# Moving GpSimd's C products, the step size's projection and the gate's Silu in a fused state-space layer

## The chip, the cores and the metric

The kernel runs on one core of a Trainium2 chip. It holds eight fused layers; the change is in the sixth part, a selective state space (Mamba-like). The metric is device time in microseconds for the whole kernel, lower is better, as the median of several runs. The core's engines are TensorE (PE; its weight loads are shown as PEld), VectorE (DVE), ScalarE (ACT), GpSimd (POOL) and SyncE (SP), which here only issues DMAs. Each engine works through its own program in order; they meet at semaphores.

## The reference, cut to what matters

The layer takes x (32 sequences of 256 positions, 128 features), normalizes it and does this:

```python
xz = xn @ W_in.T
x_inner, z = jnp.split(xz, 2, axis=-1)
...
u = jax.nn.silu(jnp.transpose(xc, (0, 2, 1)))      # xc: causal convolution, 4 taps
xbc = u @ W_x.T
dt_low, B_ssm, C_ssm = jnp.split(xbc, [DT_RANK, DT_RANK + D_STATE], axis=-1)
dt = jax.nn.softplus(dt_low @ W_dt.T + b_dt) + DT_MIN
dt = jnp.clip(dt, DT_MIN, DT_MAX)
A = -jnp.exp(log_A)
def step(h, inp):
    dA = jnp.exp(dt_t[:, :, None] * A)
    h = dA * h + (dt_t * u_t)[:, :, None] * B_t[:, None, :]
    y = jnp.einsum('bdn,bn->bd', h, C_t)
...
y = y + u * D_param
y = y * jax.nn.silu(z)
return y @ W_out.T + residual
```

There are 256 inner channels and 16 states for each channel.

## The kernel before, in words

The 8192 positions are worked off in 16 groups of 512 (two sequences). Within a group the 16 states are 16 steps, n = 0 to 15, and one step covers all 256 channels as two halves of 128 partitions, so its tiles are 128x1024.

For step n of a group:

- ACT writes the decay `dA` = exp(dt*A) with two activations (`decay`, L2363). It works two steps ahead and needs scan n-2 to be over, since `dA` has two buffers.
- POOL multiplies dt*u by the row of B, which a DMA from SP has spread over 128 partitions (`mulB`, L2202). It works two steps ahead in program order and may run up to four ahead (`inp` and `Bs` have four buffers).
- DVE scans (`h`, L2480) and multiplies by the row of C (`hc`, L2492). The row of C comes from PE: `spread_C` (L2575) writes it to `CC`, of which there is one buffer, so the spread for a step waits for DVE's C product of the step before it that uses `CC`.
- For the steps in `MOVED` (2 and 5) POOL makes the C product instead (`mulC`, L2216), from a tile `Cs` that a DMA spreads, and there is no spread on PE.
- PE adds `hc` to the two banks `Y` by a product with the identity (L2606, four matmuls).

In between, the engines prepare the next group b = g+1 (the functions `front`): PE transposes (step 1), convolves (steps 2 to 5, four matmuls in each), and projects u to the low-rank step size (`wdl`), to B and C (`wbc`), then the step size (`wdt`, two parts) and the gate z (`win`, two parts). All of these share one bank, `M`. PE's `claim(b, i)` waits until ACT has made i of the U = 9 reads of the bank for group b, counted by `m_read`. ACT's reads are, in order: xnp, u0, u1, `dtl`, then `bf`/`bc` (rows of B and C), then the two exponentials `et` of the step size, then the two halves `sz` of the gate. BF_AT and ET_AT say after which read `bf` and `et` stand.

After `bf` is read, SP stores it to DRAM (`brows`) and reads the rows back, spread, as `Bs` and `Cs`. SP's queue is in order too: at n = 9 it waits for `bf` of the next group, and the load of `Bs` for step 12 of the present group and all later ones stand behind that wait. POOL has four more jobs on the next group: `rest_of_rows` and `last_rows` (second and third bfloat16 parts of the rows of B and C), `cap` (clips the exponential) and `steps` (dt*u, and a memset of `dtA`). ACT's logarithm `Ln` waits for `cap`, `steps` waits for ACT's `dtA`, and the first decay and the first `mulB` of the next group wait for `steps`.

At the start of a group DVE also finishes the previous ones (`finish`): it adds the output of the group before last to x with its row statistics, then multiplies `Y` by the gated `sz` into `yy`, after scan 0 and before the C product of step 0. PE's diagonal products (u * D, L2603), which open the banks `Y` anew, wait for `yy`. The gate's Silu runs on ACT at step 13 (L2348), between the decays of steps 15 and 0; it needs a table load before it and one after it, since `decay` uses another table. Silu of u at step 6 (L2317) has two such loads as well.

Of the kernel before, what the change touches and what calls it, by code (L numbers as in the profile page):

```python
# [2093 lines left out]
def state_space(nc, res, name, load_next):  # L2094
# [3 lines left out]
    with ExitStack() as ctx:  # L2098
# [23 lines left out]
        MOVED = (2, 5)  # L2122
# [11 lines left out]
        U, BF_AT, ET_AT = 9, 5, 7  # L2134
        BF_FIRST, ET_FIRST = 7, 6
# [20 lines left out]
        def _(sp):  # L2156
            def step(g, k, on):
                if 1 <= g <= 6:
                    load_next(sp, g - 1)
                for n in range(N):  # L2160
                    if on(1) and n == 9:
                        wait(sp, s["m_read"], U * (g + 1) + (BF_AT if g >= 0 else BF_FIRST))
                        sp.dma_start(brows[(k + 1) % 2], bf[0:2 * N, :]).then_inc(s["b_out"], 16)
# [16 lines left out]
        def _(pool):  # L2180
            def rest_of_rows(b, j):

                wait(pool, s["m_read"], U * b + (BF_AT if b else BF_FIRST))
                wait(pool, s["rest_copied"], b)
                wait(pool, s["mulB"], N * (b - 1) + 13)
# [3 lines left out]
            def last_rows(b, j):  # L2189

                wait(pool, s["rest_copied"], b + 1)
                wait(pool, s["mulB"], N * (b - 1) + 15)
                wait(pool, s["capped"], b + 1 if b else 0)
# [32 lines left out]
            def step(g, k, on):  # L2226
                for n in range(N):
# [4 lines left out]
                    if on(1) and n == 10:  # L2232
                        rest_of_rows(g + 1, (k + 1) % 2)
                    if on(1) and n == 12:
                        last_rows(g + 1, (k + 1) % 2)
                    if on(1) and n == 11 and g >= 0:
                        cap(g + 1)
                    if on(1) and n == 13 and g >= 0:
                        steps(g + 1, (k + 1) % 2)
# [6 lines left out]
        def _(act):  # L2246
# [45 lines left out]
            def first_gate():  # L2292
                wait(act, s["m_read"], U)
                nc.scalar.activation(sz[0][:], sz[0][:], ACT.Silu).then_inc(s["sz_ready"], 1)

            def front(g, k, n):
# [24 lines left out]
                if n == 8:  # L2321
                    wait(act, s["f_mm"], U * b + 5)
# [4 lines left out]
                if n in (9, 10):  # L2327
                    c = n - 9
                    wait(act, s["f_mm"], U * b + 6 + c)
                    wait(act, s["dt_done"], b)  # L2330
                    nc.scalar.activation(et[:, c], M[:], ACT.Exp, bias=bdt[:, c:c + 1]).then_inc(s["m_read"], 1)
                if n == 12:
# [10 lines left out]
                if n == 11:  # L2343
                    wait(act, s["pseq"], b + 1)
                    nc.scalar.activation(bc[j][64:P], br[64:P], ACT.Copy).then_inc(s["rest_copied"], 1)
                if n == 13:
                    wait(act, s["m_read"], U * b + 9)
                    nc.scalar.activation(sz[j][:], sz[j][:], ACT.Silu).then_inc(s["sz_ready"], 1)  # L2348
# [17 lines left out]
            def step(g, k, on):  # L2366
                if g < 0:
                    first()
                for n in range(N):
# [8 lines left out]
                    if g == 0 and n == 1:  # L2378
                        first_gate()
# [389 lines left out]
```

## Time and profile before

| | |
|---|---|
| median of 3 runs | 4065.82 us (4064.39 to 4068.06) |
| the profiled execution: time / span | 4057.97 us / 4056.1 us |
| state-space steps, first to last scan | 2073.5 to 3038 us of the span |
| busy in that stretch (964.5 us) | DVE 879.67, PE 807.00, POOL 755.85, ACT 652.71 us |
| period of a group, start of scan 0 to the next (group 0) | 58.38 us |
| the same, groups 1 to 14 | 59.40 to 61.62 us, mean 60.79 |
| groups 2, 3, 4 | 61.16, 59.60, 60.65 us |

How to read it: the table's stretch is about a quarter of the kernel; the rest is untouched by the change. DVE is busy most, but the four engines stand close together, so the period of a group is set by who waits for whom. The group whose scan 0 starts at 2252.48 is group 3; its times are the ones shown below, and "+9.3" in the prediction means 9.3 us after its start.

### The profile page before, as it was taken

To read this page: it belongs to the slowest core of one execution; us is meant where nothing else is said; L and a number is where in the kernel's file an instruction comes from. 1 tells how busy PE (TensorE), PEld (TensorE's weight loads), DVE (VectorE), ACT (ScalarE), POOL (GpSimd) and SP (SyncE) were. 2 spreads that over 40 slices of the span, in tenths; PEclk is the share of its full clock that TensorE was granted. 3 is DMA by queue.
4 is the path that set the end of the run, shared out by engine and by line. 5 is a ranking of instruction groups with operands and counts; after the bars stand their busy time and mean duration, and the time that the engine had idled before them with its cause. 6 is when DMAs were issued, how large, how long until landed. Compare 5 with 4: busy or idle time off the path is not lost. (4 is left out here: it accounts for less than half of the span.)

```text
span 4056.1 us, 60415 instructions
## 1 busy us (share of the span) xinstructions
PE 3440.9 (85%) x21021; PEld 2133.3 (53%) x21076; DVE 2871.0 (71%) x6265; ACT 1934.2 (48%) x3530; POOL 1535.5 (38%) x999
## 2 busy tenths in 40 slices
PE   5999998969999982877668888888878999999857
PEld 3676765646777771544423333333335666666423
DVE  7888887547777746333178999999996666666575
ACT  2555555325566630322266676676652323232365
POOL 2311110632122200788747877877860000000162
PEclk9999999989999975888889999999999999999868
DMA  6333331014444433233322332222322332222101
GB/s 153 90 86 92 87 90 44 1 33 107 103 100 100 101 97 80 43 43 43 45 99 69 104 98 69 91 77 69 91 61 88 92 93 89 93 90 93 51 1 42
DMA packets 242528, 314.18 MB, mean 77 GB/s; under 512 B 46450, under 2 KB 157779, under 8 KB 231588
## 3 DMA queue, kind: packets, MB, share of 16 engines
q1 hardware_dynamic: 208308, 289.02, 26.1%
q0 software_dynamic: 22528, 17.32, 3.2%
q10 hardware_dynamic: 11392, 3.97, 0.5%
q8 instruction: 172, 2.82, 0.3%
q14 instruction: 128, 1.05, 0.1%
HBM read 251.93 MB, written 57.08 MB: 76 GB/s over the span
## 5 line engine op out<-in xcount | busy, mean ns | idle before, releaser
L574 DVE TENSOR_REDUCE a_Mx<-a_Sx 128x2 f32<-128x512 f32 (+1 forms) x1024 | 589.9, 617 | 173.1 <-PE a_Sx L626 127.2
L2202 POOL TENSOR_TENSOR a_inp<-a_dtu,a_Bs 128x1024 f32<-128x1024 f32 x256 | 598.1, 2360 | 169.9 <-DMA a_Bs<-a_brows 160.7
L2480 DVE TENSOR_TENSOR_SCAN a_h<-a_dA,a_inp 128x1024 f32<-128x1024 f32 x256 | 583.2, 2284 | 39.3 <-ACT a_dA L2363 20.4
L2606 PE MATMUL a_Y<-a_hc,g_ident 128*128 128x512 f32 x1024 | 491.6, 603 | 10.1 <-DVE a_hc L2492 5.4
L347 POOL TENSOR_TENSOR a_rest<-a_qk,a_parts 128x512 f32<-128x512 f32 x64 | 75.2, 1175 | 916.2 <-ACT a_parts L399 916.2
L2005 ACT ACTIVATE f_sg<-f_GB 128x512 f32<-128x512 f32 x272 | 162.5, 598 | 471.2 <-PE f_GB L2054 471.0
L413 ACT ACTIVATE a_Pr<-a_SA 128x512 f32<-128x512 f32 x512 | 305.4, 596 | 168.1 <-DVE a_SA L524 79.4
L623 PE MATMUL a_Sx<-att_Kp,att_Qp 96*128 96x256 bf16 (+1 forms) x2048 | 345.3, 261 | 44.2 <-DMA a_bmax<-a_lines 18.5
L2363 ACT ACTIVATE a_dA<-a_dtA,a_A 128x512 f32<-128x512 f32 x512 | 329.9, 681 | 95.7 <-DVE a_h L2480 93.9
L2080 PEld LDWEIGHTS f_OUT<-g_routed_wd,f_hm 128*128 128x128 f32 x2176 | 284.2, 191 | 138.7 <-issue 112.6
L1972 DVE TENSOR_TENSOR f_sg<-f_sg,f_UB 128x512 f32<-128x512 f32 x256 | 176.1, 688 | 233.2 <-PE f_UB L2056 210.9
L1259 POOL TENSOR_TENSOR a_root<-a_ve,a_power 128x4 f32<-128x4 f32 x16 | 16.8, 1047 | 811.2 <-DVE a_ve L1300 810.0
L2606 PEld LDWEIGHTS a_Y<-a_hc,g_ident 128*128 128x128 f32 x1024 | 197.5, 196 | 237.4 <-issue 225.8
L2492 DVE TENSOR_TENSOR a_hc<-a_h,a_CC 128x1024 f32<-128x1024 f32 x224 | 273.4, 1221 | 48.4 <-PE a_CC L2575 29.0
L2080 PE MATMUL f_OUT<-g_routed_wd,f_hm 128*128 128x128 f32 x2176 | 288.4, 276 | 6.2 <-DVE f_hm L1976 5.4
L416 ACT ACTIVATE a_Pr<-a_SB 128x512 f32<-128x512 f32 (+1 forms) x512 | 253.1, 494 | 60.4 <-PE a_SB L659 37.1
L2054 PE MATMUL f_GB<-f_xnT,g_routed_wg 128*128 128x512 f32 x544 | 281.0, 598 | 0.0
L2056 PE MATMUL f_UB<-f_xnT,g_routed_wu 128*128 128x512 f32 x544 | 278.7, 594 | 0.0
L623 PEld LDWEIGHTS a_Sx<-att_Kp,att_Qp 96*128 96x128 bf16 x2048 | 189.8, 99 | 81.3 <-DVE a_Mx L574 25.9
L1441 POOL DMA_INDIRECT f_sum<-f3e_Y,f3e_idx x128 | 202.4, 1581 | 45.4 <-issue 36.6
L1430 POOL DMA_INDIRECT f3e_xg<-f_rows,f3e_idx x128 | 125.1, 977 | 235.0 <-DVE f3e_idx L1500 196.3
L640 PE MATMUL a_SA<-att_Qp,att_Kp 128*128 128x256 bf16 x1024 | 190.2, 274 | 2.9 <-ACT a_Pr L413 0.6
(481 smaller groups left out, 6983.0 us busy)
## 6 DMA issues: line engine op xcount, KB each, us to landing
a_Bs<-a_brows SPq DMA_DIRECT2D x256, 256.0 KB, 3.3
f_Cs<-f_crows SPq DMA_DIRECT2D x512, 128.0 KB, 2.9
att_Qp<-a_packing SPq DMA_DIRECT2D x192, 192.0 KB
att_Kp<-a_packing SPq DMA_DIRECT2D x192, 192.0 KB
a_packing<-a_parts SPq DMA_DIRECT2D x64, 384.0 KB, 2.8
a_packing<-a_parts SPq DMA_DIRECT2D x64, 128.0 KB, 2.8
a_Cs<-a_brows SPq DMA_DIRECT2D x32, 256.0 KB, 3.8
g_x<-x SPq DMA_DIRECT2D x8, 512.0 KB, 7.3
```

The costliest lines, as they stand in the source:

```text
L413: nc.scalar.activation(probs[:, at:at + 2, 0:K0Q], pair(SA[j % 2], K0Q), ACT.Exp)\
L416: nc.scalar.activation(probs[:, at:at + 2, K0Q:K0Q + K1Q], pair(SB, K1Q), ACT.Exp)\
L574: nc.vector.tensor_reduce(Mx[(k + 2 - (j < LATE)) % 2][:, t, 2 * jj:2 * jj + 2], Sx[t][:, 0:2 * wd].rearrange("p (h q) -> p h q", h=2), AX ...
L623: nc.tensor.matmul(both[:, u], Qp[kb][0:KM, h, t * P:t * P + P], Kp[kb][0:KM, h, 0:wd], start=(u == 0), stop=False)
L2054: nc.tensor.matmul(GB[k][:], wg[:, q], xnT[j][:], start=True, stop=True).then_inc(s["g_mm"], 1)
L2056: nc.tensor.matmul(UB[k][:], wu[:, q], xnT[j][:], start=True, stop=True).then_inc(s["u_mm"], 1)
L2080: last = nc.tensor.matmul(OUT[j][:, t], hm[k][:, t * P:t * P + P], wd[:, q], start=False, stop=(q == NQ - 1 and t == G - 1))
L2202: nc.gpsimd.tensor_tensor(inp[n % Q][:], dtu[k][:], Bs[n % Q][:].unsqueeze(1).to_broadcast([P, CH, GT]), ALU.mult).then_inc(s["mulB"], 1)
L2363: nc.scalar.activation(dA[m % 2][:, c], dtA[k][:, c], ACT.Exp, scale=A[:, c, n:n + 1])\
L2480: nc.vector.tensor_tensor_scan(h[n % 2][:].rearrange("p c q -> p (c q)"), dA[m % 2][:].rearrange("p c q -> p (c q)"), inp[n % Q][:].rearra ...
L2492: nc.vector.tensor_tensor(hc[n % Q][:], h[n % 2][:], CC[:].unsqueeze(1).to_broadcast([P, CH, GT]), ALU.mult).then_inc(s["mulC"], 1)
L2606: nc.tensor.matmul(Y[c][:], ident[:], hc[n % Q][:, c], start=False, stop=(n == N - 1))\
```

## The change

The change alters no arithmetic. It moves work between steps and, for two C products, between engines.

- `MOVED` goes from (2, 5) to (0, 6): POOL makes the C products of steps 0 and 6, DVE those of steps 2 and 5, with their spreads on PE. PE no longer spreads C for step 0 at the end of the group before.
- PE projects the step size (`wdt`) at steps 8 and 9 and B and C (`wbc`) at step 10; before it was `wbc` at 8 and `wdt` at 9 and 10. ACT's reads follow: `et` at 8 and 9, `bf` and `bc` at 10.
- SP stores `bf` at step 11 instead of 9, so the loads behind that wait begin with the one for step 14.
- POOL's jobs: `cap` at step 10 (was 11), `rest_of_rows` 11 (was 10), `steps` 12 (was 13), `last_rows` 13 (was 12). `last_rows` now waits for `dt_ready`, the memset in `steps`.
- ACT: `Ln` and `dtA` at step 11 (was 12), ahead of the gate's first read; the copy of the rest of the rows at 12 (was 11). The gate's Silu moves from step 13 to step 6 of the group that uses it, right behind Silu of u.

```diff
--- before.py
+++ after.py
@@ -2119,7 +2119,7 @@
         h = [sc.sb(f"h{i}", [P, CH, GT]) for i in range(2)]
         hc = [sc.sb(f"hc{i}", [P, CH, GT]) for i in range(Q)]
         yy = sc.sb("yy", [P, CH, GT])
-        MOVED = (2, 5)
+        MOVED = (0, 6)
         Cs = [sc.sb(f"Cs{i}", [P, GT]) for i in range(len(MOVED))]
         diag = sc.sb("diag", [P, CH, P])
         dA = [sc.ps(f"dA{i}", [P, CH, GT]) for i in range(2)]
@@ -2131,8 +2131,7 @@
                  "dt_ready b_out cc_mm dA_done mulB scanned mulC c_in mulC_pool y_mm y_read out_mm grown summed").split()
         s = {n: sc.sem(n) for n in names}
         block = ctx.enter_context(nc.Block())
-        U, BF_AT, ET_AT = 9, 5, 7
-        BF_FIRST, ET_FIRST = 7, 6
+        U, BF_AT, ET_AT = 9, 7, 6
         b_in = [sc.sem(f"b_in{i}") for i in range(Q)]
 
         DT_MIN, DT_MAX = 0.001, 0.1
@@ -2158,8 +2157,8 @@
                 if 1 <= g <= 6:
                     load_next(sp, g - 1)
                 for n in range(N):
-                    if on(1) and n == 9:
-                        wait(sp, s["m_read"], U * (g + 1) + (BF_AT if g >= 0 else BF_FIRST))
+                    if on(1) and n == 11:
+                        wait(sp, s["m_read"], U * (g + 1) + BF_AT)
                         sp.dma_start(brows[(k + 1) % 2], bf[0:2 * N, :]).then_inc(s["b_out"], 16)
                     if on(0) if n < N - 3 else on(1):
                         if n == N - 3:
@@ -2180,17 +2179,18 @@
         def _(pool):
             def rest_of_rows(b, j):
 
-                wait(pool, s["m_read"], U * b + (BF_AT if b else BF_FIRST))
+                wait(pool, s["m_read"], U * b + BF_AT)
                 wait(pool, s["rest_copied"], b)
-                wait(pool, s["mulB"], N * (b - 1) + 13)
+                wait(pool, s["mulB"], N * (b - 1) + 14)
+                wait(pool, s["capped"], b + 1 if b else 0)
                 nc.gpsimd.tensor_tensor(br[64:P], bf[64:P], bc[j][64:P], ALU.subtract).then_inc(s["pseq"], 1)
                 wait(pool, s["pseq"], b + 1)
 
             def last_rows(b, j):
 
                 wait(pool, s["rest_copied"], b + 1)
-                wait(pool, s["mulB"], N * (b - 1) + 15)
-                wait(pool, s["capped"], b + 1 if b else 0)
+                wait(pool, s["mulB"], N * (b - 1) + 16)
+                wait(pool, s["dt_ready"], b + 1 if b else 0)
                 nc.gpsimd.tensor_tensor(bc[j][96:P], br[96:P], bc[j][96:P], ALU.subtract).then_inc(s["bc_ready"], 1)
                 wait(pool, s["bc_ready"], b + 1)
 
@@ -2229,14 +2229,14 @@
                         mulB(g * N + (n + 2), n + 2, k)
                     if n - 1 in MOVED and on(0):
                         mulC(g * N + n - 1, n - 1)
-                    if on(1) and n == 10:
+                    if on(1) and n == 10 and g >= 0:
+                        cap(g + 1)
+                    if on(1) and n == 11:
                         rest_of_rows(g + 1, (k + 1) % 2)
-                    if on(1) and n == 12:
+                    if on(1) and n == 12 and g >= 0:
+                        steps(g + 1, (k + 1) % 2)
+                    if on(1) and n == 13:
                         last_rows(g + 1, (k + 1) % 2)
-                    if on(1) and n == 11 and g >= 0:
-                        cap(g + 1)
-                    if on(1) and n == 13 and g >= 0:
-                        steps(g + 1, (k + 1) % 2)
                     if n >= N - 2 and on(1):
                         mulB(g * N + (n + 2), n + 2 - N, (k + 1) % 2)
 
@@ -2289,9 +2289,9 @@
                     wait(act, s["f_mm"], 8 + c)
                     nc.scalar.activation(sz[0][:, c], bank, ACT.Copy).then_inc(s["m_read"], 1)
 
-            def first_gate():
-                wait(act, s["m_read"], U)
-                nc.scalar.activation(sz[0][:], sz[0][:], ACT.Silu).then_inc(s["sz_ready"], 1)
+            def gate(g, k):
+                wait(act, s["m_read"], U * (g + 1))
+                nc.scalar.activation(sz[k][:], sz[k][:], ACT.Silu).then_inc(s["sz_ready"], 1)
 
             def front(g, k, n):
                 b, j = g + 1, (k + 1) % 2
@@ -2318,18 +2318,18 @@
                 if n == 7:
                     wait(act, s["f_mm"], U * b + 4)
                     nc.scalar.activation(dtl[:], M[:], ACT.Copy).then_inc(s["m_read"], 1)
-                if n == 8:
-                    wait(act, s["f_mm"], U * b + 5)
+                if n in (8, 9):
+                    c = n - 8
+                    wait(act, s["f_mm"], U * b + 5 + c)
+                    wait(act, s["dt_done"], b)
+                    nc.scalar.activation(et[:, c], M[:], ACT.Exp, bias=bdt[:, c:c + 1]).then_inc(s["m_read"], 1)
+                if n == 10:
+                    wait(act, s["f_mm"], U * b + 7)
                     wait(act, s["bc_ready"], b)
                     wait(act, s["b_out"], 16 * b)
                     nc.scalar.activation(bf[:], M[:], ACT.Copy)
                     nc.scalar.activation(bc[j][:], M[:], ACT.Copy).then_inc(s["m_read"], 1)
-                if n in (9, 10):
-                    c = n - 9
-                    wait(act, s["f_mm"], U * b + 6 + c)
-                    wait(act, s["dt_done"], b)
-                    nc.scalar.activation(et[:, c], M[:], ACT.Exp, bias=bdt[:, c:c + 1]).then_inc(s["m_read"], 1)
-                if n == 12:
+                if n == 11:
                     wait(act, s["capped"], b + 1)
                     nc.scalar.activation(et[:], et[:], ACT.Ln, bias=1.0).then_inc(s["ln_done"], 1)
                     wait(act, s["ln_done"], b + 1)
@@ -2340,12 +2340,9 @@
                     wait(act, s["y_read"], CH * g)
                     wait(act, s["f_mm"], U * b + 8 + c)
                     nc.scalar.activation(sz[j][:, c], M[:], ACT.Copy).then_inc(s["m_read"], 1)
-                if n == 11:
+                if n == 12:
                     wait(act, s["pseq"], b + 1)
                     nc.scalar.activation(bc[j][64:P], br[64:P], ACT.Copy).then_inc(s["rest_copied"], 1)
-                if n == 13:
-                    wait(act, s["m_read"], U * b + 9)
-                    nc.scalar.activation(sz[j][:], sz[j][:], ACT.Silu).then_inc(s["sz_ready"], 1)
 
             def grow_rows(g):
 
@@ -2375,8 +2372,8 @@
                         decay(g * N + (n + 2), n + 2 - N, (k + 1) % 2)
                     if on(1) and g >= 0:
                         front(g, k, n)
-                    if g == 0 and n == 1:
-                        first_gate()
+                    if on(0) and n == 6:
+                        gate(g, k)
                     if on(-1) and n == 2:
                         grow_rows(g - 1)
 
@@ -2442,7 +2439,7 @@
 
             def first():
 
-                wait(v, s["m_read"], ET_FIRST)
+                wait(v, s["m_read"], ET_AT)
                 nc.vector.tensor_scalar(et[:], et[:], CAP, 0.0, ALU.min, ALU.max).then_inc(s["capped"], 1)
                 wait(v, s["dt_done"], 1)
                 wait(v, s["u_ready"], 1)
@@ -2552,16 +2549,16 @@
                                                 start=(t == 0), stop=(t == 3))
                     if half:
                         last.then_inc(s["f_mm"], 1)
-                if n in (7, 8):
-                    i, wt = ((3, wdl), (4, wbc))[n - 7]
+                if n in (7, 10):
+                    i, wt = (3, wdl) if n == 7 else (6, wbc)
                     wait(pe, s["u_ready"], b + 1)
                     claim(b, i)
                     for c in range(CH):
                         last = nc.tensor.matmul(M[:], wt[:, c], u[j][:, c], start=(c == 0), stop=(c == CH - 1))
                     last.then_inc(s["f_mm"], 1)
-                if n in (9, 10):
-                    c = n - 9
-                    claim(b, 5 + c)
+                if n in (8, 9):
+                    c = n - 8
+                    claim(b, 4 + c)
                     nc.tensor.matmul(M[:], wdt[:, c], dtl[:], start=True, stop=True).then_inc(s["f_mm"], 1)
                 if n in (11, 12):
                     c = n - 11
@@ -2582,7 +2579,8 @@
                         spread_C(g * N + (n + 1), n + 1, k)
                     if on(1) and n == N - 1:
                         wait(pe, s["bc_ready"], g + 2)
-                        spread_C(g * N + N, 0, (k + 1) % 2)
+                        if 0 not in MOVED:
+                            spread_C(g * N + N, 0, (k + 1) % 2)
                     if on(1) and g >= 0:
                         front(g, k, n)
                     if on(-1) and n == 13:
@@ -2596,7 +2594,7 @@
                         last.then_inc(s["out_mm"], 1)
                     if on(0):
                         if n == 0 and g == 0:
-                            wait(pe, s["m_read"], BF_FIRST)
+                            wait(pe, s["m_read"], BF_AT)
                         if n == 0:
                             wait(pe, s["y_read"], CH * g)
                             for c in range(CH):
```

## Rows read from the trace of the kernel before

**Rows 1.** Groups of instructions by line, 2073.5 to 3038 us (columns: busy us, mean ns | idle before).
```profile
L2480 DVE TENSOR_TENSOR_SCAN a_h<-a_dA,a_inp 128x1024 f32<-128x1024 f32 x256 | 583.2, 2284 | 39.3 <-ACT a_dA L2363 20.4 <-POOL a_inp L2202 16.6
...
L2492 DVE TENSOR_TENSOR a_hc<-a_h,a_CC 128x1024 f32<-128x1024 f32 x224 | 273.4, 1221 | 48.4 <-PE a_CC L2575 29.0 <-DMA f3e_xg<-f_rows,f3e_idx 5.1
...
L2216 POOL TENSOR_TENSOR a_hc<-a_h,a_Cs 128x1024 f32<-128x1024 f32 x32 | 75.3, 2353 | 20.4 <-DVE a_h L2480 20.4
...
L2348 ACT ACTIVATE a_sz<-a_sz 128x1024 f32<-128x1024 f32 x15 | 15.9, 1057 | 0.2
```

**Rows 2.** The waits of the same stretch (us in total, times, longest).
```profile
POOL a_inp L2202 <- DMA a_Bs<-a_brows: 160.7, 15, 11.0
...
PE a_Y L2603 <- DVE a_hc L2492: 34.2, 6, 5.8
```

**Rows 3.** DVE in order of time: scan 0 of groups 1, 15; group 3.
```profile
2131.92 2.29 DVE L2480 TENSOR_TENSOR_SCAN a_h<-a_dA,a_inp 128x1024 f32<-128x1024 f32 x1 [1.31 <-POOL a_inp L2202]
...
2252.48 2.29 DVE L2480 TENSOR_TENSOR_SCAN a_h<-a_dA,a_inp 128x1024 f32<-128x1024 f32 x1 [1.35 <-POOL a_inp L2202]
...
2257.36 1.21 DVE L2492 TENSOR_TENSOR a_hc<-a_h,a_CC 128x1024 f32<-128x1024 f32 x1
...
2285.65 2.29 DVE L2480 TENSOR_TENSOR_SCAN a_h<-a_dA,a_inp 128x1024 f32<-128x1024 f32 x1 [0.34 <-ACT a_dA L2363]
...
2312.08 2.29 DVE L2480 TENSOR_TENSOR_SCAN a_h<-a_dA,a_inp 128x1024 f32<-128x1024 f32 x1 [1.34 <-POOL a_inp L2202]
...
2982.98 2.29 DVE L2480 TENSOR_TENSOR_SCAN a_h<-a_dA,a_inp 128x1024 f32<-128x1024 f32 x1 [1.45 <-ACT a_dA L2363]
```

**Rows 4.** POOL in order of time, from the end of group 2 to group 4.
```profile
2249.99 13.92 POOL L2202 TENSOR_TENSOR a_inp<-a_dtu,a_Bs 128x1024 f32<-128x1024 f32 x6
...
2293.69 2.36 POOL L2202 TENSOR_TENSOR a_inp<-a_dtu,a_Bs 128x1024 f32<-128x1024 f32 x1 [10.71 <-DMA a_Bs<-a_brows]
...
2301.01 2.37 POOL L2202 TENSOR_TENSOR a_inp<-a_dtu,a_Bs 128x1024 f32<-128x1024 f32 x1
...
2309.59 11.60 POOL L2202 TENSOR_TENSOR a_inp<-a_dtu,a_Bs 128x1024 f32<-128x1024 f32 x5
```

**Rows 5.** ACT in order of time, group 3.
```profile
2278.70 0.69 ACT L2314 ACTIVATE a_u<-a_M,g_state_cbias 128x512 f32<-128x512 f32 x1 [3.88 <-PE a_M L2551]
...
2288.67 0.60 ACT L2325 ACTIVATE a_bf<-a_M 128x512 f32<-128x512 f32 x1 [1.41 <-PE a_M L2560]
...
2300.27 1.28 ACT L2334 ACT_TABLE_LOAD   x1
...
2305.60 1.30 ACT L2363 ACTIVATE a_dA<-a_dtA,a_A 128x512 f32<-128x512 f32 x2
```

**Rows 6.** PE in order of time, group 3.
```profile
2258.63 0.61 PE L2575 MATMUL a_CC<-a_bc,g_state_sel 128*128 128x512 bf16 x1 [5.26 <-DVE a_hc L2492]
...
2261.90 1.88 PE L2606 MATMUL a_Y<-a_hc,g_ident 128*128 128x512 f32 x4
...
2276.72 1.88 PE L2551 MATMUL a_M<-a_xnp,g_state_cw 128*128 128x512 f32 x4
...
2286.76 1.88 PE L2560 MATMUL a_M<-a_u,g_state_wbc 128*128 128x512 f32 x4
```

**Rows 7.** PE in order of time: expert choice, group 2, and the later gated recurrence.
```profile
1884.00 0.66 PE L1555 MATMUL f3e_T<-g_ident,f3e_xg 128*128 128x128 f32 x4 [2.40 <-DMA f3e_xg<-f_rows,f3e_idx]
...
2201.28 2.90 PE L2606 MATMUL a_Y<-a_hc,g_ident 128*128 128x512 f32 x4
...
3857.00 0.66 PE L1326 MATMUL a_T<-g_ident,a_xn 128*128 128x128 f32 x4 [1.71 <-ACT a_xn L1247]
3858.34 1.68 PE L1330 MATMUL a_Z<-a_xnT,g_gru_wz 128*128 128x512 f32 x2 [0.69 <-ACT a_xnT L1227]
3859.82 1.91 PE L1332 MATMUL a_HH<-a_xnT,g_gru_wh 128*128 128x512 f32 x2
```

**Rows 8.** Stretches of 1.5 us, PE alone: length, busy, granted clock, DMA share, GB/s.
```profile
2195.82:2197.32 1.50, 0.00 (x0) 0.72 0.34 83
...
2201.82:2203.32 1.50, 1.50 (x3) 0.50 0.43 127
2203.32:2204.82 1.50, 1.50 (x7) 1.00 0.52 124
```

## The prediction, made before the changed kernel had run

> **What bounds the kernel now.** I read the groups of instructions by line first. A scan takes 2.28 us and DVE's C product 1.22 [rows 1], so a step costs DVE 3.51, and a step in `MOVED` 2.23. With 14 of the one, 2 of the other and 2.50 for `finish` (the rest of scan 0 to the C product, 4.88 in [rows 3]) a group would take DVE 56.1 us. The starts of scan 0 in groups 1 and 15 stand 851.06 us apart, 14 periods of 60.79 [rows 3]. So 4.7 us of each group are waits of DVE, and they are all that the change can win: 14 x 4.7 = 66 us, 1.6%.
>
> Then I read the waits. DVE waits for `CC`, for ACT's decays and for POOL's `inp`, none of them dominant [rows 1]. POOL waits 10.7 us a group for `Bs` [rows 2, 4], which looks like a big loss; but group 3 in order of time shows that POOL had run ahead there, and that the loss is what follows: from 2293.69 on it makes five B products and four other jobs without a gap, and scan 0 of the next group starts at 2312.08, right behind the last [rows 3, 4]. About 1.35 us are lost there. ACT ends its decays at the same moment (in group 15 it is the one that DVE waits for [rows 3]), so relief for POOL alone would give nothing.
>
> The middle of a group is bound by PE. It sits idle 5.26 us at the start of a group, until DVE's C product 0 frees `CC` [rows 6] (in some groups the idle time, up to 5.8, is booked on the diagonal products [rows 2]), then it has 3.66 us of work a step (Y 1.72, spread 0.22, convolution 1.72) against DVE's 3.51 until the convolution ends, and u, Silu and decay 9 hang on that.
>
> **The change part by part**, in us after the start of group 3 (2252.48), at full PE clock first.
>
> *C product 0 on POOL.* DVE drops 1.22 behind `finish`, so scan 1 could start at +4.9 and scan 2 at +8.4. But POOL's program has it behind B products 1, 2 and 3. POOL paces 2.32 a product (13.92/6 [rows 4]) and takes 2.35 for the C product [rows 1]. The end of B product 0 is about the start of the group, so C product 0 ends at 3 x 2.32 + 2.35 = +9.3, and scan 2 (same `h` buffer) starts at +9.35: 1.0 late. In the last group nothing else binds: scan 0 to scan 15 took 6.0 + 12 x 3.51 + 2 x 2.23 = 52.6 and takes 9.35 + 12 x 3.51 + 2.23 = 53.7 now.
>
> *PE.* No spread of C for step 0, and the spread for 1 runs early. But `Y` for step 0 needs POOL's product: it starts at +9.35, before at 2261.90, +9.42 [rows 6]. From there PE is busy without a gap. To the last half convolution (2276.72) it took 14.82 [rows 6]; the new order has the spreads for 2 and 5 and not the one for 6, net one more of 0.22. So this comes at +24.4, before at +24.24. Nothing is won: PE's early idle time stays.
>
> *The gate's Silu at step 6.* u follows the convolution by 1.98 (2276.72 to 2278.70), and scan 9 follows that by 6.95 (to 2285.65) [rows 3, 5, 6]; the gate's 1.06 [rows 1] is now in this chain: scan 9 starts at 24.4 + 1.98 + 6.95 + 1.06 = +34.4 (before +33.17). It needs no table load of its own. In DVE's own order scan 9 would be due at +32.9, so nothing covers the 1.06: it is paid in full. What is saved is at step 13: 1.06 and two loads of 1.28 (one load lasts 1.28 in [rows 5]).
>
> *The projections.* Reordering costs no work. C product 10 ends 7.1 after scan 9 starts (two steps and 0.1), the spread takes 0.3, and `bf` follows the start of its product by 1.91 (2286.76 to 2288.67 [rows 5, 6]): `bf` at +34.4 + 9.3 = +43.7, before +36.2.
>
> *The end of the group by POOL.* `bf` to the first B product behind it is 5.02 (2288.67 to 2293.69 [rows 4, 5]); SP's queue is moved past the loads for 12 and 13, so it is now the one for 14. From there POOL has B product 14, `steps`, 15, `last_rows`, 0: the same work as from 2301.01 to 2309.59 [rows 4], plus 2.36. 43.7 + 5.0 + 8.6 + 2.4 = +59.7. The new wait of `last_rows` is for `steps`, in front of it on the same engine: nothing. B products 12 and 13 are no longer behind SP's wait; that helps no scan, they were in time.
>
> *The end by ACT.* Behind `bf` come its twin and decay 13 (2.3 together), then load, `Ln`, `dtA`, half a gate, load, decay: as from 2300.27 to 2305.60, 5.33 [rows 5]; the scan starts 1.39 later. Scan 14 at 43.7 + 2.3 + 5.3 + 1.4 = +52.7, two steps of 3.51 to scan 0: +59.7. In DVE's own order scan 14 would have come at +52.0.
>
> So at full clock the period is 59.7. Group 3 had 59.60. The losses have changed places: 1.35 to 1.0 at the boundary (there now by C product 0), 1.5 at scan 9, 0.7 at scan 14, 0.3 at C product 7, which still waits for its spread. These chains lean on neighbours within 0.1 us; I allow 0.3 either way.
>
> *The clock.* Group 2 shows what PE's idle time does: the clock falls to 1.2 GHz (0.50) while PE is idle and returns at 2203.3, some 5.8 after PE's restart [rows 8], and the four Y matmuls take 2.90 instead of 1.88 [rows 6, 7]. Group 3 got the clock back earlier and its period is 1.56 shorter than that of group 2. What does the new order do? PE works until about +2, idles 2.9 until `yy` frees the banks, does 1.7 of diagonal products, idles 2.6 until +9.35. No row has this pattern. From one side: after a single idle time of 2.40 between long work the transposes took 0.66, full clock (half is 1.1) [rows 7]. From the other: in the gated recurrence, idle times of 1.71 and 0.69 around a short product were enough: the next two matmuls took 1.68 and 1.91 where full clock gives 1.02 [rows 7]. Two gaps with a short piece of work between are nearer to the second. I take it that the clock falls in most groups. Before, the low clock covered the spread, the diagonals and part of Y 0; now PE restarts in earnest at +9.35, and the low stretch lies on Y 0, spread 2, the transposes and Y 1, all of them on the chain to scan 9 and with C product 2 of DVE waiting for spread 2. I take half speed for 3.4 us of that work, between none and group 2's 5.8: it costs half of it, 1.7, with bounds 0 and 2.9. Period 59.65 + 1.7 = 61.35.
>
> The Trainium skill (TensorE: Matmul & The Clock Gate, "HAM oscillation — how this bites in real kernels") describes loops that wait once in every tile and start every tile cold, and advises fewer, shorter waits. By the letter of it, splitting one wait of 5.3 into 2.9 and 2.6 would keep the clock up, and the period would be 59.65; the rows of the recurrence speak against it, and I keep it as a rival.
>
> **The sum.** Groups 1 to 14: 14 x (61.35 - 60.79) = +7.8. Group 0 had 58.38, since no group before it had to be finished; now its scan 2 waits for POOL at +9.35 all the same, and its clock is down from the start: about 61.4, +3. Group 15: the 1.1 above, and spread 2 at low clock makes C product 2 later by another 1.1 (Y 0 and the spread take 1.9 at full clock, some 1.2 more at the low one): +2.2. The gate's Silu in group 15 brings two loads of its own, hidden, since ACT there has 2.2 us free a step. Sum +13; to this I add 1 for what the low clock does in a group that loses more than the mean: +14 us. On its own execution: 4057.97 + 14 = 4072. The median of the runs is 7.9 above that execution, so 4080.
>
> **Rivals.**
> - *The clock stays up.* For it: no single idle time is over 2.9 us, and one of 2.40 did no harm [rows 7]. Then 14 x (59.65 - 60.79) = -16, group 0 +1.3, group 15 +1: -14, or 4052. It decides at a mean cost of the clock of 0.7 us a group or less.
> - *Nothing moves beyond the measurement.* My full-clock period is 0.4 too high (decay 9 and both tails come sooner) and the clock costs 1.4: a period of 60.65, 14 x (60.65 - 60.79) + 4 for groups 0 and 15 = +2, or 4068. That the gate and the projections only swap one wait for another speaks for it.
> - *The queue of SP becomes the bound.* `bf` is 7.5 us later, and behind it the loads for 14, 15, 0, 1 and both `Cs` come in one burst, with the store that the load for 0 waits for. Before, they had 7 us more. If `Bs` 14 lands 1 us later than 5.02 after `bf`, POOL's tail has no slack to hide it, and each group pays 1: 14 + 14 = +28, 4094. Against it: B product 0 is due 11 us after `bf`, and only the first load is tight.
>
> **How the numbers follow.** The chance of the forecast (4072 to 4090, its own range) is 0.6, the clock that stays up 0.16, nothing moves 0.14, SP's queue 0.1. The forecast's low end, clock 1.2 and period 60.9, is +6, so a small part of it falls within 0.2% (8 us, about what a measurement of this kernel tells from no change). Slower 0.66, same 0.18, faster 0.16. The range leaves out most of the rival that is faster and the far end of SP's: 4060 to 4094. Predicted 4080.
>
> **What would show it.** Right: scan 2 starts about 9.35 after scan 0 and waits for POOL's C product 0; scan 9 waits for decay 9 by 1 to 3 us; the wait of POOL for `Bs` is at B product 14 and short; scans 13 and 15 don't wait for POOL; the Y 0 matmuls take 2.5 to 3.4 for four, and the granted clock is 0.50 there. DVE's wait for `inp` vanishes from the table, and its waits for POOL's `hc` and for `dA` grow. Wrong: full clock at +9.4, and periods of 59.6; or C product 0 done before +8.4, which would need POOL ahead of the group's start.

## The result, and the profile after

The changed kernel takes 4081.13 us (median of 7 runs, 4077.33 to 4083.5), the kernel before in the same comparison 4066.75 (7 runs): a ratio of 1.0034, 95% interval 1.0022 to 1.0046, 0.34% slower. The profiled execution took 4083.5 us with a span of 4081.7, 25.6 more than that of before. Not all of it is the change: scan 0 of group 0 starts at 2083.28 instead of 2073.54, so 9.7 us had already passed in earlier stages, whose code is the same (other executions below start between 2071 and 2086). From the start of the first scan to the start of the last the stage took 974.95 us, before 961.94: 13.0 more.

DVE in order of time in the changed kernel: scan 0 of groups 1, 7, 8 and 15, and what lies between in group 7 (answers to [rows 3]).

```profile
2145.36 2.29 DVE L2477 TENSOR_TENSOR_SCAN a_h<-a_dA,a_inp 128x1024 f32<-128x1024 f32 x1 [0.17 <-POOL a_inp L2202]
...
2514.41 2.29 DVE L2477 TENSOR_TENSOR_SCAN a_h<-a_dA,a_inp 128x1024 f32<-128x1024 f32 x1 [0.17 <-POOL a_inp L2202]
...
2519.29 2.28 DVE L2477 TENSOR_TENSOR_SCAN a_h<-a_dA,a_inp 128x1024 f32<-128x1024 f32 x1
...
2523.70 2.29 DVE L2477 TENSOR_TENSOR_SCAN a_h<-a_dA,a_inp 128x1024 f32<-128x1024 f32 x1 [0.81 <-POOL a_hc L2216]
2527.45 1.22 DVE L2489 TENSOR_TENSOR a_hc<-a_h,a_CC 128x1024 f32<-128x1024 f32 x1 [1.47 <-PE a_CC L2572]
...
2550.23 2.29 DVE L2477 TENSOR_TENSOR_SCAN a_h<-a_dA,a_inp 128x1024 f32<-128x1024 f32 x1 [1.29 <-ACT a_dA L2360]
...
2568.55 2.29 DVE L2477 TENSOR_TENSOR_SCAN a_h<-a_dA,a_inp 128x1024 f32<-128x1024 f32 x1 [0.68 <-ACT a_dA L2360]
...
2575.84 2.29 DVE L2477 TENSOR_TENSOR_SCAN a_h<-a_dA,a_inp 128x1024 f32<-128x1024 f32 x1 [0.17 <-POOL a_inp L2202]
...
3004.04 2.29 DVE L2477 TENSOR_TENSOR_SCAN a_h<-a_dA,a_inp 128x1024 f32<-128x1024 f32 x1
```

(3004.04 - 2145.36) / 14 = 61.33 us is the mean period of groups 1 to 14; it was 60.79. From scan 0 to scan 9 a group now takes 35.76 on the mean, before 34.26; from scan 9 to the next scan 0 it takes 25.58, before 26.53. So 1.50 is lost in the first part and 0.95 won in the second. Group 7 (61.43) shows the waits that are left: 0.8 for POOL's C product 0 at scan 2, 1.5 for the spread at C product 2, 1.3 at scan 9, 0.7 at scan 14, and at scan 0 only 0.17 where group 3 had 1.35 before. The waits at C products 3 and 6 of before (0.96 and 1.04 a group) are gone.

PE in the same group, in order of time (answers to [rows 6]), and PE alone in stretches of 1.5 us (length, busy, granted clock, DMA share, GB/s; answers to [rows 8]).

```profile
2519.43 3.21 PE L2601 MATMUL a_Y<-a_u,a_diag 128*128 128x512 f32 x4 [3.09 <-DVE a_yy L2459]
2523.62 3.58 PE L2604 MATMUL a_Y<-a_hc,g_ident 128*128 128x512 f32 x4 [0.98 <-POOL a_hc L2216]
2527.04 0.38 PE L2572 MATMUL a_CC<-a_bc,g_state_sel 128*128 128x512 bf16 x1
...
2540.36 1.88 PE L2548 MATMUL a_M<-a_xnp,g_state_cw 128*128 128x512 f32 x4
```

```profile
2517.41:2518.91 1.50, 0.00 (x0) 1.00 0.34 130
2518.91:2520.41 1.50, 0.98 (x2) 0.88 0.30 104
2520.41:2521.91 1.50, 1.50 (x3) 0.50 0.50 116
...
2526.41:2527.91 1.50, 1.50 (x8) 0.85 0.39 123
```

The one idle time of 5.3 has become two, of 3.09 and 0.98. The clock falls all the same, to 0.50 (1.2 GHz), during the diagonal products, which then take 3.21 (1.98 where the clock stays up, in a run below) and fill most of the second gap. It comes back within the stretch from 2526.41. Y 0 starts 9.21 after scan 0 and its four matmuls take 3.58; the last half convolution starts at +25.95. The clock isn't low for longer than before: over groups 1 to 14 its mean is 0.95 in both kernels. But before it fell while PE was still idle [rows 8], and now it falls in groups 2 to 13 with PE at work, 5.6 to 6.2 after scan 0, so more of the low stretch lies on work.

POOL and ACT in the same group, in order of time (answers to [rows 4] and [rows 5]).

```profile
2511.97 9.28 POOL L2202 TENSOR_TENSOR a_inp<-a_dtu,a_Bs 128x1024 f32<-128x1024 f32 x4
2521.21 2.35 POOL L2216 TENSOR_TENSOR a_hc<-a_h,a_Cs 128x1024 f32<-128x1024 f32 x1
...
2564.80 2.36 POOL L2202 TENSOR_TENSOR a_inp<-a_dtu,a_Bs 128x1024 f32<-128x1024 f32 x1 [2.94 <-DMA a_Bs<-a_brows]
...
2569.66 2.37 POOL L2202 TENSOR_TENSOR a_inp<-a_dtu,a_Bs 128x1024 f32<-128x1024 f32 x1
```

```profile
2542.34 0.69 ACT L2314 ACTIVATE a_u<-a_M,g_state_cbias 128x512 f32<-128x512 f32 x1 [3.10 <-PE a_M L2548]
...
2545.53 1.06 ACT L2317 ACTIVATE a_u<-a_u 128x1024 f32<-128x1024 f32 x1
2546.49 1.04 ACT L2294 ACTIVATE a_sz<-a_sz 128x1024 f32<-128x1024 f32 x1
2547.55 1.28 ACT L2360 ACT_TABLE_LOAD   x1
...
2559.54 0.60 ACT L2330 ACTIVATE a_bf<-a_M 128x512 f32<-128x512 f32 x1 [2.18 <-PE a_M L2557]
...
2567.16 1.30 ACT L2360 ACTIVATE a_dA<-a_dtA,a_A 128x512 f32<-128x512 f32 x2
```

POOL makes four B products without a gap (9.28) and only then C product 0, which ends at 2523.56, +9.15. On ACT the gate's Silu stands between Silu of u and the table load that decay 9 waits for.

### The profile page after: what moved, and what is told of

Its sections match the earlier page's. It is cut to its first block and busy times, and to the rows that moved or that the text cites. A ratio compares the mean times of both kernels' runs of the same rounds, so it can differ in the third digit from the quotient of the medians.

```text
span 4081.7 us, 60400 instructions
## 1 busy us (share of the span) xinstructions
PE 3467.9 (85%) x21021; PEld 2125.8 (52%) x21076; DVE 2871.4 (70%) x6265; ACT 1896.0 (46%) x3500; POOL 1535.9 (38%) x999
## 3 DMA queue, kind: packets, MB, share of 16 engines
q1 hardware_dynamic: 208308, 289.02, 26.1%
## 5 line engine op out<-in xcount | busy, mean ns | idle before, releaser
L2604 PE MATMUL a_Y<-a_hc,g_ident 128*128 128x512 f32 x1024 | 510.0, 622 | 51.0 <-POOL a_hc L2216 30.1
L1259 POOL TENSOR_TENSOR a_root<-a_ve,a_power 128x4 f32<-128x4 f32 x16 | 16.6, 1037 | 812.9 <-DVE a_ve L1300 811.8
L416 ACT ACTIVATE a_Pr<-a_SB 128x512 f32<-128x512 f32 (+1 forms) x512 | 253.0, 494 | 60.3 <-PE a_SB L659 37.1
```

Of the source, the lines that this page charges most:

```text
L416: nc.scalar.activation(probs[:, at:at + 2, K0Q:K0Q + K1Q], pair(SB, K1Q), ACT.Exp)\
L2604: nc.tensor.matmul(Y[c][:], ident[:], hc[n % Q][:, c], start=False, stop=(n == N - 1))\
```

## The experiments

Each kernel was timed beside the kernel before on the same chip. The chips differ (the kernel before takes 4055.36 us on one and 4071.09 on another), so the ratio to before is what is compared. Differences between two ratios of under about 0.15%, or 6 us, are within what the intervals leave open. "Period" is the mean of groups 1 to 14 in the run's own profile.

| kernel | ratio to before (95%) | period |
|---|---|---|
| C products 0 and 6 alone | 1.0022 (1.0013 to 1.0031) | 60.80 |
| gate's Silu alone | 1.0020 (1.0011 to 1.0029) | 61.20 |
| projections alone | 0.9959 (0.9945 to 0.9972) | 59.72 |
| changed, gate back | 0.9990 (0.9981 to 0.9999) | 60.23 |
| changed, C products back | 1.0000 (0.9991 to 1.0009) | 61.03 |
| changed, projections back | 1.0030 (1.0019 to 1.0041) | 61.11 |
| the changed kernel | 1.0034 (1.0022 to 1.0046) | 61.33 |
| changed, PE kept busy | 0.9977 (0.9968 to 0.9986) | 59.77 |
| changed, C product 0 early | 0.9938 (0.9924 to 0.9951) | 58.46 |
| early, PE kept busy | 0.9922 (0.9908 to 0.9935) | 58.48 |
| early, gate at step 13 | 0.9923 (0.9909 to 0.9936) | 58.28 |
| early, gate at step 2 | 0.9906 (0.9891 to 0.9921) | 58.01 |
| early, gate at step 2, PE busy | 0.9883 (0.9868 to 0.9898) | 57.52 |

**The clock: PE kept busy.**

```diff
+                if n == 1:
+                    for _ in range(9):
+                        nc.tensor.matmul(CC[:], sel[:, N + n], bc[k][:], start=True, stop=True)
...
-                            for c in range(CH):
-                                nc.tensor.matmul(Y[c][:], diag[:, c], u[k][:, c], start=True, stop=False)
+                            for last in (False, True):
+                                for c in range(CH):
+                                    nc.tensor.matmul(Y[c][:], diag[:, c], u[k][:, c], start=True, stop=not last)
```

> The changed kernel with PE kept at work in its two idle times at the start of a group: the spread of C for step 1 is made ten times and the diagonal products twice, with the same values written again. Nothing is left out. Theory: the granted clock stays at 1.00 through the start of the group, PE's chain from +9.2 is 1.7 us shorter, DVE no longer waits for the spread of step 2, and the period falls to 59.7 us: 4056 to 4060 us. Rival (the low clock is a symptom, GpSimd's product and ACT set the period): the clock stays up and the time stays at 4078 to 4084 us.

It is 0.23% faster than before, 0.57% faster than the changed kernel (23 us), and the period is 59.77. PE of this kernel in group 7 (scan 0 at 2494.43), in order of time, and two stretches of 4 us with their granted clock:

```profile
2499.45 3.70 PE L2605 MATMUL a_Y<-a_u,a_diag 128*128 128x512 f32 x8 [0.93 <-DVE a_yy L2459]
2503.65 1.98 PE L2608 MATMUL a_Y<-a_hc,g_ident 128*128 128x512 f32 x4 [0.51 <-POOL a_hc L2216]
```

```profile
2494.43:2498.43 4.00, 4.00 (x14) 1.00 0.30 102
2498.43:2502.43 4.00, 3.07 (x8) 1.00 0.43 100
```

Y 0 starts at the same place, +9.22, and takes 1.98 instead of 3.58. So the low clock, and not PE's start, costs the changed kernel 61.33 - 59.77 = 1.56 us a group, and more matmuls, done for nothing, made it faster. What it cost the kernel before was not measured: PE was not kept busy there. Its groups 3 and 9, which got the clock back early, have periods of 59.60 and 59.70, the other twelve 60.98 on the mean, so it cost over 1 us a group there too. The 1.56 is a price within the changed kernel, and only a part of it can be a difference to before.

**GpSimd's order: C product 0 ahead of B product 3.**

```diff
+                    if n == 1 and on(0):
+                        mulC(g * N, 0)
                     if n < N - 2 and on(0):
                         mulB(g * N + (n + 2), n + 2, k)
-                    if n - 1 in MOVED and on(0):
-                        mulC(g * N + n - 1, n - 1)
+                    if n == 7 and on(0):
+                        mulC(g * N + 6, 6)
```

> The changed kernel with one order turned on GpSimd: the C product of step 0 ahead of the B product of step 3 instead of behind it. Theory: that C product ends at +7.0 instead of +9.2, PE restarts there, scan 2 starts in DVE's own order at +8.4, scan 9 at about 32.1 plus the clock's cost instead of 34.4 plus 1.7; a period of 58.5 to 59.5 us and 4045 to 4055 us in all, better than both kernels. Rival (B product 3, now later, or the chain of bf and GpSimd's tail sets the period): no gain or under 0.5 us a group, 4074 to 4081 us.

With this one order turned the kernel is 25 us faster than before and nearly 40 faster than the changed one. POOL, then PE of group 7 (scan 0 at 2481.48):

```profile
2479.04 6.99 POOL L2202 TENSOR_TENSOR a_inp<-a_dtu,a_Bs 128x1024 f32<-128x1024 f32 x3
2485.98 2.35 POOL L2216 TENSOR_TENSOR a_hc<-a_h,a_Cs 128x1024 f32<-128x1024 f32 x1
```

```profile
2486.50 1.98 PE L2603 MATMUL a_Y<-a_u,a_diag 128*128 128x512 f32 x4 [2.90 <-DVE a_yy L2461]
2488.39 1.98 PE L2606 MATMUL a_Y<-a_hc,g_ident 128*128 128x512 f32 x4
```

C product 0 ends at 2488.33, +6.85; Y 0 follows the diagonal products at once, and DVE waits neither at scan 2 nor at C product 2. In this group the clock stays up through an idle time of 2.90. In six of groups 1 to 14 it falls, around idle times of 2.63 to 2.93; in the other eight it stays up, seven of them with 2.61 to 2.95. Over 2073.5 to 2960 us it is 0.98, in the changed kernel 0.94, so part of this gain is the clock's. The period of 58.5 to 59.5 and the 11 to 21 us under before that I expected were missed on the fast side.

**Each part alone, and each taken out.** The C products alone, on the kernel before:

```diff
-        MOVED = (2, 5)
+        MOVED = (0, 6)
...
-                        spread_C(g * N + N, 0, (k + 1) % 2)
+                        if 0 not in MOVED:
+                            spread_C(g * N + N, 0, (k + 1) % 2)
```

> The kernel before with one part of the change: GpSimd makes the C products of steps 0 and 6 instead of 2 and 5. Theory (the C product of step 0 stands behind three B products in GpSimd's queue, so PE restarts at +9.2 with its clock down and everything up to scan 9 shifts): scan 9 at about +35, and from there the old tail of 26.4 us: a period of 61.3 to 61.4 us and 4076 to 4081 us in all, so this part alone makes the whole loss. Rival (the gate's Silu at step 6 and the later bf make the loss, the C products are neutral): 4064 to 4068 us, period 60.8.

Slower by 0.22%, 9 us, but the reason I gave holds in part only. The period stayed at 60.80, as the rival had it: scan 2 does wait for C product 0 (0.83 a group) and C product 2 for its spread (0.96), but the waits at C products 3 and 6 are gone. Eight groups take over 61; in the others, of 59.4 to 60.3, C product 2 waits 0.54 at most. The loss in this profile is outside the mean: group 0 took 62.43 instead of 58.38, and group 15 about 1.7 more, 5.9 in the whole stage. It doesn't make the whole loss.

The gate alone (on the kernel before, the Silu moved from step 13 to 6):

```diff
-                if n == 13:
-                    wait(act, s["m_read"], U * b + 9)
-                    nc.scalar.activation(sz[j][:], sz[j][:], ACT.Silu).then_inc(s["sz_ready"], 1)
...
+                    if on(0) and n == 6:
+                        gate(g, k)
```

> The kernel before with only the gate's Silu moved to step 6. Theory: scan 9 and with it bf come 1.0 us later, GpSimd's tail from bf on (23.4 us to scan 0) is unchanged and binds alone, so the table loads freed on ACT give nothing: the period grows by 0.9 to 1.1 us, 12 to 16 us slower than before. Rival (the end of the group is bound by ACT): the freed 3.6 us are worth more than the 1.06, and it is faster than before.

Slower by 0.20%, 8 us, less than the 12 to 16 expected. Scan 9 did come 0.9 later in its group, but the end of the group gave 0.5 back (26.02 from scan 9 to scan 0, before 26.53): scan 0 had waited for ACT in six groups of fourteen, now it does in one. DVE in order of time at the end of group 7, scans 15 and 0; scan 0 waits for POOL:

```profile
2566.91 2.29 DVE L2477 TENSOR_TENSOR_SCAN a_h<-a_dA,a_inp 128x1024 f32<-128x1024 f32 x1 [0.18 <-ACT a_dA L2360]
2571.53 2.29 DVE L2477 TENSOR_TENSOR_SCAN a_h<-a_dA,a_inp 128x1024 f32<-128x1024 f32 x1 [1.02 <-POOL a_inp L2202]
```

The projections alone, with the queue orders and waits that belong to them; of the diff:

```diff
-        U, BF_AT, ET_AT = 9, 5, 7
+        U, BF_AT, ET_AT = 9, 7, 6
...
-                if n in (7, 8):
-                    i, wt = ((3, wdl), (4, wbc))[n - 7]
+                if n in (7, 10):
+                    i, wt = (3, wdl) if n == 7 else (6, wbc)
```

> The kernel before with only the projections moved, and the queue orders that go with them: C products on GpSimd at 2 and 5, gate's Silu at step 13. Theory from the runs so far (the two parts measured without it are both slower than before, the runs with it gain on them): the part from scan 9 to the next scan 0 takes 25.9 us, as in the run with the gate moved back, instead of 26.4, and the period falls by 0.5 us, 6 to 10 us faster than before. Rival (the prediction's reading, one wait swapped for another): no change, within 4 us of before.

They are a gain of 0.41%, 17 us, twice what I expected and far from the "no change" of the prediction's reading. DVE of this kernel, the end of group 7, in order of time:

```profile
2531.70 2.29 DVE L2480 TENSOR_TENSOR_SCAN a_h<-a_dA,a_inp 128x1024 f32<-128x1024 f32 x1 [0.34 <-ACT a_dA L2363]
...
2550.03 2.29 DVE L2480 TENSOR_TENSOR_SCAN a_h<-a_dA,a_inp 128x1024 f32<-128x1024 f32 x1 [0.68 <-ACT a_dA L2363]
2553.71 2.29 DVE L2480 TENSOR_TENSOR_SCAN a_h<-a_dA,a_inp 128x1024 f32<-128x1024 f32 x1
2557.62 2.29 DVE L2480 TENSOR_TENSOR_SCAN a_h<-a_dA,a_inp 128x1024 f32<-128x1024 f32 x1 [0.30 <-ACT a_dA L2363]
```

Scan 9 (2531.70) to the next scan 0 takes 25.92, before 26.43 (2285.65 to 2312.08 [rows 3]); over groups 1 to 14 this part is 0.59 of the 1.07 us a group. Scan 0 doesn't wait for POOL any more. The other 0.48 lies before scan 9, mostly at C product 3, and goes with PE's clock: every second group of this run has a period of about 59.2, no wait at C product 3 and a granted clock of 0.89 over its first 15 us; those between have 60.3, a wait of about 1 and 0.77. Before, twelve of the fourteen groups had 0.77. Why the clock alternates here was not tested.

Then each part taken out of the changed kernel, by the lines shown above turned round. The gate back at step 13:

```diff
-                    if on(0) and n == 6:
-                        gate(g, k)
+                    if g == 0 and n == 1:
+                        first_gate()
```

> The changed kernel with the gate's Silu back at step 13, between two table loads. Theory: scan 9 comes 1.06 us sooner, but the end of the group on ACT (decay 15, load, Silu, load, decay 0) then ends at about +59.0 plus what the clock costs, instead of 59.7: 0.3 to 0.7 us a group less, 4070 to 4077 us. Rival (the gate's place is the cause): all 15 us come back, 4066 us or less. Rival (it is fully covered): 4081 us.

0.44% less than the changed kernel, 18 us, where the theory expected 4 to 11; it is the rival's time. In the profile the place of the gate costs 0.94 at scan 9 and gives 0.36 back behind it (25.94 to 25.58); another 0.52 of the difference lies ahead of scan 8, where the granted clock over the first 15 us of a group is 0.84 here and 0.79 in the changed kernel. The C products back at 2 and 5:

```diff
-        MOVED = (0, 6)
+        MOVED = (2, 5)
```

> The changed kernel with the C products of GpSimd back at steps 2 and 5; projections, queue orders and the gate's Silu stay as changed. Theory (C product 0 on GpSimd is the larger part of the loss; the gate at step 6 costs 1.0 us at scan 9 and what it frees at the group's end just about pays for it): mean period 60.4 to 60.8, 0 to 7 us faster than the kernel before. Rival (projections and gate carry a loss of their own): a period over 61, 4 us or more slower than before.

Level with before, the slow edge of the theory, though the period of 61.03 is the rival's. With scan 9 late by the gate (step 8 is 4.88 in each group), what the projections win is used up in this run. And the projections back, with the other two parts as in their own runs:

> The changed kernel without the projections' part: C products 0 and 6 on GpSimd and the gate's Silu at step 6, projections and queue orders as before. Theory (the projections are a gain wherever they are made, here as in the run with them alone): from scan 9 to the next scan 0 25.9 us as with the gate moved alone, instead of 25.5, so the period goes from 61.3 of the changed kernel to 61.6 to 61.9, 18 to 24 us slower than before. Rival (the projections only gain while the gate's Silu is at step 13): as the changed kernel, 12 to 15 us slower than before.

Here the theory failed. The part from scan 9 on is 0.5 us longer, as expected, but the period is 61.11 and the time 0.30% over before, 12 us: as the changed kernel. So the projections gain 17 us alone, 13 beside the C products (1.0022 to 0.9990), 8 beside the gate (1.0020 to 1.0000) and nothing clear beside both (1.0030 to 1.0034). The profiles show where it went. Without the projections the part behind scan 9 is 0.56 longer (26.14), but the part ahead of it is 0.79 shorter (34.97 instead of 35.76), and the granted clock over the first 15 us of a group is 0.83 instead of 0.79.

**A version that beats both.** With C product 0 early (the diff above), first the ten spreads in addition, without the second pair of diagonal products:

> C product 0 ahead of B product 3 on GpSimd, and the spread of C for step 1 made ten times to keep PE at work until the diagonal products. Theory: in the run with the early product alone PE's chain to the last half convolution is 0.1 to 0.5 us late from the low clock; with the clock up the wait for the spread of step 7 is gone and the period is 58.2 instead of 58.46: 2 to 4 us less than with the early product alone, 27 to 30 us faster than before. Rival (the clock still costs about 1 us there): 15 us less.

No gain in the period (58.48 to 58.46): the clock is up, the wait at step 7 is gone, and the part behind scan 9 takes it back (25.67 instead of 25.45), with 0.18 a group at scan 0 for POOL. The ratio is 0.16% lower, but the intervals overlap. With the clock up in both, the early C product is worth 59.77 - 58.48 = 1.29 us a group; the rest of its 2.87 (61.33 to 58.46) is the clock.

Then the gate back at step 13 instead:

> C product 0 ahead of B product 3 on GpSimd, projections as changed, gate's Silu at step 13 as before. Theory: scan 9 is 1.0 us sooner than with the gate at step 6, the part behind it 25.9 us instead of 25.3, so a period of 57.9 to 58.2 and 36 to 40 us faster than before, level with the gate at step 2. Rival (two table loads more at the group's end bind again): 58.5 or more, no better than the early product alone.

58.28, and 31 us faster than before by the ratio, a little under the 36 to 40 expected: the groups that keep the clock have 57.85 or 57.95 (the first of them 56.75), the others 58.1 to 60.1. And the gate at step 2:

> C product 0 ahead of B product 3 on GpSimd, and the gate's Silu at step 2, between decay 4 and decay 5, with two table loads of its own; the four scalings of x move from step 2 to step 3. ACT idles there, so 3.6 us fit before decay 5 is due. Theory: scan 9 waits 0.2 instead of 1.24 for its decay, and the period goes from 58.46 to 57.4 to 57.6: some 38 to 42 us faster than before. Rival (ACT is late with u0, PE waits for it at the second convolution, and the gain is given back): 58.3 to 58.8, no better than the early product alone.

```diff
-                    if on(0) and n == 6:
+                    if on(0) and n == 2:
                         gate(g, k)
-                    if on(-1) and n == 2:
+                    if on(-1) and n == 3:
                         grow_rows(g - 1)
```

38 us faster, as expected, though the period is 58.01 and not 57.5: C product 7 now waits 0.53 for its spread, and scan 8 comes 0.44 late. Last, the ten spreads added to that:

> Early C product 0, gate's Silu at step 2, and the spread of C for step 1 made ten times so that PE keeps its clock. Theory: the step from scan 7 to scan 8, 3.90 us with the gate at step 2, loses most of its 0.4 of waiting only if it is PE's clock; then 57.7 and 3 to 5 us less than without. Rival (it is u0, late behind the gate on ACT): the step stays at 3.9, the period at 58.0.

57.52 and 0.9883, 48 us faster than before; by the ratios that is 9 us better than without the spreads, where 3 to 5 were expected. The step from scan 7 to 8 went from 3.93 to 3.49, so that wait was the clock's. DVE's waits over the stage in this kernel (us in total, times, longest); before, it waited 20.4 for ACT's `dA`, 16.6 for POOL's `inp` and 29.0 for `CC` [rows 1]:

```profile
DVE a_h L2479 <- ACT a_dA L2362: 11.2, 19, 0.7
...
DVE a_h L2479 <- POOL a_inp L2202: 7.6, 21, 3.4
...
DVE a_hc L2491 <- PE a_CC L2577: 2.5, 3, 1.9
```

## Why the prediction was right, and where it was not

- *C product 0 behind three B products.* Right. Forecast end +9.3, scan 2 at +9.35; measured +9.15 and +9.29 (2523.70). The run with the order turned shows that this place in POOL's queue is the cause of the wait: there it is gone.
- *The clock.* Right, and tested directly. I took 1.7 us a group at full price, from rows that were only near; with PE kept busy the difference is 1.56. The last half convolution was due at 24.4 + 1.7 = +26.1 and came at +25.95. The full-clock period was to be 59.65 and is 59.77. That the sum meets 61.33 so closely is luck in part, since these two errors cancel, and Y 0 took 3.58, beyond the 2.5 to 3.4 that I gave as the sign. The rival that the clock stays up, and with it the Trainium skill's advice (TensorE: Matmul & The Clock Gate, "HAM oscillation — how this bites in real kernels") taken by the letter, fell here: it stood at 0.50 after the first idle time, of 3.09. I had drawn the low stretch as lying on Y 0 and what follows; it began earlier, on the diagonal products. In the rows of the recurrence I took 1.02 as the full-clock time of both products; the first takes 1.12 (3830.25 in the trace of before), which changes nothing in the argument. What the runs don't settle is when exactly a pause costs the clock: with the early product, idle times of 2.6 to 2.9 did in six groups and not in seven others.
- *The gate's Silu.* Right in place: scan 9 at +35.82 (2550.23), where 34.4 + 1.7 = +36.1 was due. It "is paid in full" there, 0.95. The prediction gives the place no price as a whole, and one chain doesn't show it: 8 us alone, 18 us on top of the other two parts.
- *The projections.* The sum has one figure for the end of the group, gate and projections together: 59.7 - 34.4 = 25.3 from scan 9 to scan 0, where the rows had 26.43. It came out as 25.58, before 26.53. What was missed is their weight: "Reordering costs no work" and "the losses have changed places" leave them no price of their own, and alone they are worth 17 us, the largest of the three parts. A little over half of that is the end of the group, where POOL no longer holds up scan 0; the rest is ahead of scan 9 and goes with the clock. The total came out all the same, because beside the other two parts they gain nothing.
- *SP's queue.* `bf` to B product 14 took 5.26 (2559.54 to 2564.80), forecast 5.0. POOL waited 2.94 for it, and what follows holds scan 0 up by 0.17 only. The rival, a loss of 1 in each group, fell.
- *The ends of the stage.* Group 0 took 62.08, forecast 61.4. In group 15 the clock was up at the start, so the 1.1 for the spread of step 2 was not there. It fell later, around an idle time of PE of 2.47 before Y 6 (granted clock 0.79 over 3028 to 3036 us): the four matmuls took 3.60 instead of 1.98, C product 8 waited 0.69 for its spread, and scan 9 came 0.6 late. The gate's two loads did stay hidden: with PE kept busy they stand there too, and that step takes 3.51. So the 2.2 for this group came near its 1.7 by luck. Sum in the profile: group 0 +3.7, groups 1 to 14 +7.6, group 15 +1.7, in all +13.0, where the forecast had +3, +7.8, +2.2 and a reserve of 1.

The parts don't add: alone they are +0.22, +0.20 and -0.41%, together +0.34. What the profiles show is that PE's clock changes with them: up to scan 8 a group takes 0.79 longer in the changed kernel than without the projections, though their moved work starts only at step 8, and the granted clock is lower. That the clock is what hides the gain is argued from this and was not tested; it would take the same kernels with PE kept busy.

## What to carry to other kernels

Moving work to an idle engine pays only if its place in that engine's queue is early enough for the first consumer: the same C product one B product sooner turned 0.34% slower into 0.62% faster. Time the parts of a combined change one by one; here the best of three was hidden by the other two. When the matrix engine idles for a few microseconds once in every loop, price the low clock that follows, and try idle matmuls into a bank that is rewritten anyway.

## What the runs showed of the hardware

- Redundant matmuls made the kernel faster: 9 more spreads and 2 more diagonal products a group, some 4 us of extra PE work, gave 1.56 us a group back through the clock (granted clock over 2073.5 to 2960 us 1.00 instead of 0.94).
- The mean granted clock doesn't tell what it costs: it is 0.95 over groups 1 to 14 both before and after, but before it fell in PE's idle time and after it falls on the diagonal products.
- Splitting one idle time of 5.3 us into 3.1 and 1.0 did not keep the clock up (group 7: 0.50 from 2520.41 to 2521.91 us).
- The same untouched earlier stages put the first scan anywhere from 2071.0 to 2085.8 us in the profiled executions, so a single profile's span says little on a change of 10 us; the stage's own first-to-last-scan time does.
